# One addition in a kernel's setup: an immediate replaced by a tensor of ones

## The chip, the cores and the metric

The kernel runs on one core of one Trainium2 chip. The metric is the device time of one execution in microseconds. Timed runs of the kernel before: 690.28 us in the median of 3 runs, from 690.0 to 690.36.

## The reference, cut to what matters

A small language model tower on 64 sequences of 128 tokens, width 256: an attention layer on embedded tokens, then a gated linear recurrence, then a linear layer with the signs of a weight. The edit lies in what is computed from log_decay, the recurrence's decay.

```python
h = tok_attention(emb[x], Wq, bq, Wk, bk, Wv, bv, Wo, bo)      # 16 heads of 16
xn = layernorm(h)
Bu_proj = (xn @ B_w.T) @ C_w.T
decay = sigmoid(log_decay)                                     # (256,)
state = exclusive_scan(decay, Bu_proj)                         # over the 128 tokens
h = h + sigmoid(xn @ gate_w.T + gate_b) * state
h = h + layernorm(h) @ sign(ffn_weight).T
```

The sigmoid is computed as 1 / (1 + exp(-log_decay)), on a tile of 128 partitions x 2 columns that holds the 256 features.

## The kernel before, in words

The kernel takes the 64 sequences in 32 pairs. A software pipeline of turns runs over the pairs: turn t computes the scores and probabilities of pair t in 8 steps, while the projections of pair t+1, the context of pair t-1, the recurrence of pair t-2 and the last layer of pairs t-3 and t-4 are placed between the steps. Every engine has its own queue, written out by hand in the program's order, with semaphores between the engines; no planner changes it. Turns -2 to 5 and the last six are written out, the others are a loop.

Ahead of the turns, and inside turns -1 and 0, lies the setup. What matters here, by engine:

- **VectorE** clears small tiles (L500 to L504: powers, zero_col, eps_col and two v_wide), wraps and clips the token ids (L509 to L513) and hands them to TensorE, which turns them, and then to GpSimd (tok_ids, L515). It makes low parts of the weights wk, wq, wv (L519, L523) and centres wo. In turn -1, turn_weights follows (L539 to L557): a copy of bo_turned, the addition of one to exp(-log_decay) (L543), the reciprocal that gives decay (L545), two scans that give its powers (L549), the low part of wo (L519), a comparison of the last weight with zero (L555, with an immediate, from SBUF to SBUF) and its signs (L557). Behind it in the same queue come k_low and q_low of pair 0 (L642), gate_row (L562), state_row (L567) and the first maxima (L583).
- **GpSimd** waits for the ids, gathers embedding rows (L309), and in turns -2 and -1 clears k_stack and q_stack of one parity each (L365, L366), then copies the id columns of the next pair (L299) and gathers again.
- **ScalarE** computes exp(-log_decay) in turn_weights (L397), the high parts of weights (L382, among them woh), and k_high and q_high (L468, L480).
- **TensorE** makes the k and q features of pair 0, then in prepare (ahead of turn 0) transposes the powers (L777), waits for k_low of pair 0, and folds the centred wo into two weights: 24 matmuls, called the fold below. Then come the first scores.
- **SyncE** queues the transfers that spread k_high, k_low, q_high and q_low over k_stack and q_stack (L262, L267), each behind its part, in that order.

Of the kernel before, what the change touches and what calls it, by code (L numbers as in the profile page):

```python
# [32 lines left out]
ALU = mybir.AluOpType  # L33
# [8 lines left out]
P = 128  # L42
C = D // P
# [15 lines left out]
def build(nc, x, emb, wqT, bq, wkT, bk, wvT, bv, woT, bo, b_w, c_wT, gate_wT, gate_b, log_decay, ffn_wT, out):  # L59
    ctx = ExitStack()  # L60
    with ctx:  # L61
        def sb(name, shape, dt=fp32):
            return ctx.enter_context(nc.sbuf_tensor(name, shape, dt))
# [4 lines left out]
        def sem(name):  # L68
            return ctx.enter_context(nc.semaphore(name))
# [12 lines left out]
        e_ld, e_ld1, decay = sb("e_ld", [P, C]), sb("e_ld1", [P, C]), sb("decay", [P, C])  # L82
# [3 lines left out]
        earlier_raw, earlier = sb("earlier_raw", [P, SEQ]), sb("earlier", [P, SEQ], f32r)  # L86
        ones_col = sb("ones_col", [P, 2])
        gb_row = sb("gb_row", [P, D])
        zero_col, eps_col = sb("zero_col", [P, 1]), sb("eps_col", [P, 2])
        bv_rows, bo_row = sb("bv_rows", [P, 2, D]), sb("bo_row", [P, D])  # L90
        x_raw = sb("x_raw", [BATCH, SEQ], i32)
        x_wrap, x_sum, x_clip = (sb(n, [BATCH, SEQ]) for n in ("x_wrap", "x_sum", "x_clip"))
# [6 lines left out]
                                for n in ("xT", "ctxT", "h1T"))  # L99
# [60 lines left out]
        ids_turned, ids_ready, wstate_mm, prep_step, prep_done = (sem("ids_turned"), sem("ids_ready"), sem("wstate_mm"),  # L160
                                                      sem("prep_step"), sem("prep_done"))
# [4 lines left out]
        earlier_made, dve_gate, eps_made = sem("earlier_made"), sem("dve_gate"), sem("eps_made")  # L166
# [332 lines left out]
        def _(dve):  # L499
            nc.vector.memset(powers[:, :, 0:1], 0.5).then_inc(prep_step, 1)  # L500
            nc.vector.memset(zero_col[:], 0.0).then_inc(prep_step, 1)
            nc.vector.memset(eps_col[:], EPS).then_inc(eps_made, 1)
            for par in range(2):
                nc.vector.memset(v_wide[par][:], 0.0).then_inc(prep_step, 1)  # L504
            dve.wait_ge(prep_step, 4)
            dve.wait_ge(eps_made, 1)

            dve.wait_ge(x_loaded, 16)
            nc.vector.tensor_scalar(x_wrap[:], x_raw[:], 0.0, float(VOCAB), ALU.is_lt, ALU.mult).then_inc(ids_step, 1)  # L509
# [7 lines left out]
            def low_part(part, src, n):  # L517
                dve.wait_ge(w_high, n)
                nc.vector.tensor_tensor(part[1][:], src, part[0][:].bitcast(fp32), ALU.subtract).then_inc(w_low, 1)  # L519
# [19 lines left out]
            def turn_weights():  # L539
                dve.wait_ge(wo_flipped, 1)  # L540
                nc.vector.tensor_copy(bo_turned[:, :, 0:P], ps_t[:, D:2 * D].rearrange("p (k f) -> p k f", k=C)).then_inc(turned_copied, 1)
                dve.wait_ge(exp_ld, 1)
                nc.vector.tensor_scalar(e_ld1[:], e_ld[:], 1.0, None, ALU.add).then_inc(prep_step, 1)  # L543
                dve.wait_ge(prep_step, 5)
                nc.vector.reciprocal(decay[:], e_ld1[:]).then_inc(prep_step, 1)  # L545
                dve.wait_ge(prep_step, 6)
                for c in range(C):

                    nc.vector.tensor_tensor_scan(powers[:, c, 1:SEQ], decay[:, c:c + 1].to_broadcast([P, SEQ - 1]),  # L549
                                                 zero_col[:].to_broadcast([P, SEQ - 1]), powers[:, c, 0:1],  # L550
                                                 ALU.mult, ALU.add).then_inc(powers_made, 1)
                low_part(wo, raw[0][:], 4)
                dve.wait_ge(raw_loaded[2], 32)
                dve.wait_ge(w_low, 4)
                nc.vector.tensor_scalar(raw[0][:], raw[2][:], 0.0, None, ALU.is_lt).then_inc(prep_step, 1)  # L555
                dve.wait_ge(prep_step, 7)
                nc.vector.scalar_tensor_tensor(wf_sign[:], raw[2][:], 0.0, raw[0][:], ALU.is_gt,  # L557
                                               ALU.subtract).then_inc(prep_done, 1)
# [17 lines left out]
            def turn(t, par):  # L576
# [129 lines left out]
                if exists(t + 1):  # L706
                    if isinstance(t, int) and t == -1:
                        turn_weights()
                    split_low(k_low, g3, bk_col, k_high, act_khi, dve_klo)
# [287 lines left out]
```

## Time and profile before

| | |
|---|---|
| median of the timed runs | 690.28 us |
| profiled execution | 690.76 us |
| its span, first to last instruction | 688.7 us |
| TensorE (PE) matmul busy | 628.8 us, 91% |
| VectorE (DVE) busy | 616.4 us, 89% |
| ScalarE (ACT) busy | 592.2 us, 86% |
| GpSimd (POOL) busy | 428.4 us, 62% |
| mean granted TensorE clock | 0.988 |

The busy shares are means over the whole span. The setup lies in the first 35 us, where the shares are lower than in the steady part. Times in rows of the trace are in microseconds from the start of the span; a granted clock of 1.00 is 2.4 GHz and one of 0.50 is 1.2 GHz.

### The profile page before, as it was taken

Reading aid. Unit: us, or ns where it says so; the run is one execution under the profiler, and the core shown is the slowest. Engines: PE = TensorE matmul, PEld = TensorE weight load, DVE = VectorE, ACT = ScalarE, POOL = GpSimd, SP = SyncE. Lnnn points to the kernel's source line nnn. Section 1 sums busy time; section 2 is a strip of 40 time slices with the busy share of each in tenths; the row PEclk is TensorE's granted clock in tenths of the full one; section 3 lists DMA queues with packets and bytes.
Section 4 is the critical chain, followed back from the end, with each engine's and each line's share of the span. In section 5 each row is a group of like instructions: output and inputs, shape, how many; then the busy total and the mean of one; then the engine's idle time right before and its main releaser. Section 6 shows DMA issues by size and latency. Waiting matters only on the chain. (4 is left out here: it accounts for less than half of the span.)

```text
span 688.7 us, 21152 instructions
## 1 busy us (share of the span) xinstructions
PE 628.8 (91%) x6633; PEld 593.6 (86%) x6633; DVE 616.4 (89%) x1343; ACT 592.2 (86%) x2219; POOL 428.4 (62%) x464
## 2 busy tenths in 40 slices
PE   3678999999999999999999999999999999999772
PEld 2567989999999999999999999999999999999662
DVE  5666899999999999999999999999999999999893
ACT  3199999999999999999999999999999999999810
POOL 7401567666667676666676676666676776665595
PEclk9899999999999999999999999999999999999997
DMA  5323322233333322233443322333344322333000
GB/s 154 115 93 108 109 80 91 93 109 109 124 122 122 122 78 91 92 104 122 122 122 122 105 84 91 100 107 122 122 122 122 84 89 90 103 122 109 17 32 31
DMA packets 56162, 69.81 MB, mean 101 GB/s; under 512 B 6785, under 2 KB 41793, under 8 KB 56129
## 3 DMA queue, kind: packets, MB, share of 16 engines
q1 hardware_dynamic: 52048, 60.48, 26.8%
q0 software_dynamic: 3072, 8.39, 5.5%
q10 hardware_dynamic: 1008, 0.53, 0.3%
q8 instruction: 17, 0.28, 0.2%
q14 instruction: 17, 0.13, 0.1%
HBM read 10.65 MB, written 8.39 MB: 28 GB/s over the span
## 5 line engine op out<-in xcount | busy, mean ns | idle before, releaser
L420 ACT ACTIVATE probs<-ps_s,neg_max 128x128 f32<-128x128 f32 x1024 | 343.6, 400 | 11.4 <-DVE neg_max L583 11.4
L583 DVE TENSOR_REDUCE neg_max<-ps_s 128x4 f32<-128x512 f32 x256 | 175.6, 686 | 33.0 <-PE ps_s L750 28.9
L430 ACT COPY probsT<-ps_t 128x512 f32<-128x512 f32 x256 | 162.4, 634 | 15.9 <-PE ps_t L850 15.9
L850 PE MATMUL ps_t<-ident,probs 128*128 128x128 f32 x1024 | 156.1, 275 | 11.7 <-ACT probsT L430 10.1
L420 ACT ACTIVATION_READ_ACCUMULATOR probs<-ps_s,neg_max 128x1 f32 x640 | 157.3, 246 | 0.0
L850 PEld LDWEIGHTS ps_t<-ident,probs 128*128 128x128 f32 x1024 | 114.0, 141 | 20.5 <-issue 8.9
L750 PE MATMUL ps_s<-k_stack,q_stack 128*128 128x256 f32 x512 | 123.9, 323 | 0.0
L323 POOL TENSOR_TENSOR h<-gated,h 128x512 f32<-128x512 f32 x32 | 41.0, 1283 | 82.5 <-DVE gated L659 47.4
L360 POOL TENSOR_TENSOR mean_part<-sign_row,mean_scaled 128x512 f32<-128x512 f32 x32 | 33.3, 1041 | 93.9 <-DVE mean_scaled L736 93.8
L750 PEld LDWEIGHTS ps_s<-k_stack,q_stack 128*128 128x128 f32 x512 | 77.4, 191 | 0.1
L309 POOL DMA_INDIRECT x_emb<-in_emb,id_col x64 | 66.2, 1035 | 15.6 <-issue 14.3
L616 DVE TENSOR_REDUCE row_sum<-probs 128x4 f32<-128x512 f32 x96 | 64.7, 674 | 0.0
L750 PE MATMUL ps_c<-probsT,v_wide 128*32 128x128 f32 x2048 | 62.5, 274 | 0.0
L328 POOL TENSOR_TENSOR inv_wide<-inv_sum,ones_col 128x512 f32<-128x512 f32 x32 | 33.2, 1038 | 43.7 <-DVE inv_sum L625 28.5
L750 PEld LDWEIGHTS ps_c<-probsT,v_wide 128*32 128x32 f32 x2048 | 53.9, 110 | 4.4
L750 PE MATMUL ps_g<-woh,ctxTh 128*128 128x256 f32 x128 | 39.1, 305 | 15.3 <-DVE ctxTl L723 15.3
L598 DVE BATCH_NORM_STATS2 stats<-h 128x6 f32<-128x256 f32 x128 | 47.8, 415 | 3.4 <-POOL h L323 2.3
L315 POOL TENSOR_TENSOR rs<-ve,neg_half 128x2 f32<-128x2 f32 x64 | 46.5, 726 | 5.2 <-DVE ve L610 4.4
L750 PEld LDWEIGHTS ps_g<-woh,ctxTh 128*128 128x128 f32 x128 | 24.0, 187 | 22.8 <-DVE ctxTl L723 22.8
L356 POOL TENSOR_TENSOR state_low<-state_in,state_high 128x512 fp32r<-128x512 f32 x32 | 41.6, 1301 | 2.5
L342 POOL TENSOR_TENSOR gate_bias<-gate_bias,gb_row 128x512 f32<-128x512 f32 x32 | 41.4, 1294 | 2.5
L363 POOL TENSOR_TENSOR y_rest<-h,mean_part 128x512 f32<-128x512 f32 x32 | 41.3, 1291 | 2.5
(148 smaller groups left out, 1929.8 us busy)
## 6 DMA issues: line engine op xcount, KB each, us to landing
k_stack<-k_high SPq DMA_DIRECT2D x128, 128.0 KB, 3.5
q_stack<-q_high SPq DMA_DIRECT2D x64, 256.0 KB, 2.5
k_stack<-k_low SPq DMA_DIRECT2D x64, 128.0 KB, 3.4
q_stack<-q_low SPq DMA_DIRECT2D x32, 256.0 KB, 2.4
out<-y SPq DMA_DIRECT2D x32, 256.0 KB
x_emb<-in_emb,id_col POOLq DMA_INDIRECT x64, 3.9
raw<-in_wkT SPq DMA_DIRECT2D x1, 256.0 KB, 3.5
raw<-in_wqT SPq DMA_DIRECT2D x1, 256.0 KB, 4.2
```

The lines of the kernel that those rows point to most:

```text
L309: nc.gpsimd.indirect_dma_start(x_emb[par][b][:], None, emb, bass.IndirectOffsetOnAxis(ap=id_col[par][b][:], axis=0)).then_inc(gathered[par ...
L315: nc.gpsimd.tensor_tensor(rs[:], ve[:], neg_half[:], ALU.pow).then_inc(rs_done, 1)
L342: nc.gpsimd.tensor_tensor(gate_bias[:], gate_bias[:], gb_row[:].unsqueeze(1).to_broadcast([P, 2, D]), ALU.add).then_inc(pool_bias, 1)
L356: nc.gpsimd.tensor_tensor(state_low[:], state_in[:], state_high[:].bitcast(fp32), ALU.subtract).then_inc(state_lows, 1)
L363: nc.gpsimd.tensor_tensor(y_rest[:], h1[:], mean_part[:], ALU.subtract).then_inc(pool_rest, 1)
L420: last = nc.scalar.activation(probs[s % 2][:, j], ps_s[s % 2][:, j * SEQ:j * SEQ + SEQ], ACT.Exp, bias=neg_max[s % 2][:, j:j + 1], accum_o ...
L430: nc.scalar.copy(probsT[st][vp if st < AHEAD else 0][:], ps_t[:]).then_inc(act_pT, 1)
L583: nc.vector.tensor_reduce(neg_max[s % 2][:], ps_s[s % 2][:].rearrange("p (h k) -> p h k", h=HPS), axis=AX.X, op=ALU.max, negate=True).then ...
L598: nc.vector.bn_stats(stats[:, b], h[:, b]).then_inc(done_st, 1)
L616: nc.vector.tensor_reduce(row_sum[par][:, s // 4, s % 4 * HPS:s % 4 * HPS + HPS], probs[s % 2][:], axis=AX.X, op=ALU.add).then_inc(dve_sum, 1)
L750: return nc.tensor.matmul(dst, lhsT, rhs, start=first, stop=last)
L850: last = nc.tensor.transpose(ps_t[:, j * SEQ:j * SEQ + SEQ], probs[st % 2][:, j], ident[:])
```

## The change

A tile unit_col of 128 x 2 is added and filled with ones by a memset on VectorE, ahead of the two v_wide memsets. The wait for eps_made, behind them, is raised from 1 to 2. The addition of one at L543 is written as tensor_tensor of e_ld and unit_col instead of tensor_scalar of e_ld with the immediate 1.0. Tiles that are allocated behind unit_col may lie at other addresses.

```diff
-        zero_col, eps_col = sb("zero_col", [P, 1]), sb("eps_col", [P, 2])
+        zero_col, unit_col, eps_col = sb("zero_col", [P, 1]), sb("unit_col", [P, C]), sb("eps_col", [P, 2])
...
             nc.vector.memset(eps_col[:], EPS).then_inc(eps_made, 1)
+            nc.vector.memset(unit_col[:], 1.0).then_inc(eps_made, 1)
             for par in range(2):
                 nc.vector.memset(v_wide[par][:], 0.0).then_inc(prep_step, 1)
             dve.wait_ge(prep_step, 4)
-            dve.wait_ge(eps_made, 1)
+            dve.wait_ge(eps_made, 2)
...
                 dve.wait_ge(exp_ld, 1)
-                nc.vector.tensor_scalar(e_ld1[:], e_ld[:], 1.0, None, ALU.add).then_inc(prep_step, 1)
+                nc.vector.tensor_tensor(e_ld1[:], e_ld[:], unit_col[:], ALU.add).then_inc(prep_step, 1)
                 dve.wait_ge(prep_step, 5)
```

## Rows read from the trace of the kernel before

**Rows 1.** Stretches: PE, PEld, DVE, ACT, POOL busy (count), clock, DMA share, GB/s.

```profile
200.00:220.00 20.00, 19.48 (x210) 18.32 (x208) 18.89 (x42) 18.79 (x73) 12.90 (x14) 1.00 0.37 115
```

**Rows 2.** Order of time, VectorE's first instructions: start, duration, engine, line, operation.

```profile
0.93 0.06 DVE L502 MEMSET eps_col<- 128x2 f32 x1
...
2.32 0.96 DVE L504 MEMSET v_wide<- 128x1088 f32 x1 [0.18 <-issue]
3.32 0.22 DVE L509 TENSOR_SCALAR x_wrap<-x_raw 64x128 f32<-64x128 int32 x1
```

**Rows 3.** Order of time, the edited instruction and its followers; two ScalarE producers.

```profile
16.14 5.87 DVE L543 TENSOR_SCALAR e_ld<-e_ld 128x2 f32<-128x2 f32 x1
16.28 0.62 ACT L382 CAST woh<-raw 128x512 fp32r<-128x512 f32 x1
...
17.84 0.84 ACT L468 ACTIVATE k_high<-ps_g,bk_col 128x256 fp32r<-128x256 f32 x2 [0.94 <-PE ps_g L750]
...
22.05 0.17 DVE L545 RECIPROCAL decay<-e_ld 128x2 f32<-128x2 f32 x1
...
23.02 0.67 DVE L519 TENSOR_TENSOR wol<-raw,woh 128x512 fp32r<-128x512 f32 x1
...
23.79 0.48 DVE L555 TENSOR_SCALAR raw<-raw 128x512 f32<-128x512 f32 x1
...
24.92 0.87 DVE L642 SCALAR_TENSOR_TENSOR k_low<-ps_g,bk_col,k_high 128x256 fp32r<-128x256 f32 x2
```

**Rows 4.** Order of time, GpSimd beside the edited instruction.

```profile
16.70 3.54 POOL L365 MEMSET k_stack<- 128x4096 f32 x1
...
20.17 1.82 POOL L366 MEMSET q_stack<- 128x2048 f32 x1
...
21.92 0.31 POOL L299 COPY id_col<-tok_ids 128x1 int32<-128x1 int32 x2
```

**Rows 5.** Order of time, VectorE beside GpSimd elsewhere; last, all of L610 (min/median/max ns).

```profile
8.43 3.54 POOL L365 MEMSET k_stack<- 128x4096 f32 x1
...
10.49 0.69 DVE L519 TENSOR_TENSOR wvl<-raw,wvh 128x512 fp32r<-128x512 f32 x1 [2.87 <-ACT wvh L382]
...
90.03 1.28 POOL L323 TENSOR_TENSOR h<-gated,h 128x512 f32<-128x512 f32 x1 [9.04 <-DVE gated L659]
90.05 1.28 DVE L610 TENSOR_TENSOR ve<-mv,eps_col 128x2 f32<-128x2 f32 x1
...
382.34 1.28 POOL L323 TENSOR_TENSOR h<-gated,h 128x512 f32<-128x512 f32 x1 [2.55 <-DVE gated L659]
382.57 0.35 DVE L625 RECIPROCAL inv_sum<-row_sum 128x32 f32<-128x32 f32 x1
...
L610 DVE TENSOR_TENSOR ve<-mv,eps_col x64: 160/161/1281, 70.5 to 679.5; 128x2 f32<-128x2 f32 x64
```

**Rows 6.** Order of time, TensorE from the powers to the first scores; SyncE's last stack transfer.

```profile
23.16 0.44 PE L777 MATMUL ps_t<-ident,powers 128*128 128x128 f32 x2 [3.99 <-DVE powers L549]
...
25.94 3.75 PE L750 MATMUL ps_c<-raw,gate_in 128*128 128x256 f32 x8 [2.34 <-DVE k_low L642]
...
28.37 0.61 SPq L267 DMA_DIRECT2D q_stack<-q_low  x1
...
33.30 0.59 PE L750 MATMUL ps_s<-k_stack,q_stack 128*128 128x256 f32 x2
```

**Rows 7.** Stretches of TensorE alone: PE busy (count), granted clock, DMA share, GB/s.

```profile
19.00:23.10 4.10, 0.17 (x2) 1.00 0.42 128
...
25.94:30.90 4.96, 4.96 (x12) 0.53 0.66 226
30.90:33.30 2.40, 2.40 (x13) 1.00 0.00 0
```

**Rows 8.** Transfers into q_stack, first 60 us: issue to landing.

```profile
DMA to landing us min/median/max: 2.4/2.7/3.1
```

**Rows 9.** Waits from 12 to 40 us: total, times, longest.

```profile
ACT wgh L382 <- PE ps_g L750: 11.1, 1, 11.1
```

## The prediction

> **What bounds the kernel now.** I read the stretches of equal length first. In the middle of the run TensorE is busy 19.48 of 20 us, VectorE 18.89 and ScalarE 18.79 [rows 1]; the edited instruction isn't there. It runs once, in the setup, so the steady part doesn't change its pace and the question is by how much it starts sooner or later. For that I read the order of time of the first 35 us, engine by engine, then the waits there.
>
> In the setup one row stands out: the addition on 2 elements per partition takes 5.87 us, from 16.14 to 22.01 [rows 3], where the reciprocal of the same shape behind it takes 0.17 [rows 3] and a tensor_tensor of that shape in the loop has a median of 0.161 [rows 5]. No engine is named as what it waits for; the time is inside the instruction. Beside it GpSimd clears k_stack and q_stack of the other parity without a gap, 16.70 to 20.24 and 20.17 to 21.99 [rows 4]. The addition ends 0.02 us behind the second memset. So it is held by GpSimd's memsets, and asked before they began but did not get through.
>
> Who waits for it? VectorE's queue goes on in order: reciprocal, scans, wo's low part, comparison L555, signs L557, then k_low at 24.92 [rows 3]. TensorE's fold (the 24 matmuls of prepare) starts at 25.94 and its wait of 2.34 us is ended by k_low [rows 6]. The powers' transposes at 23.16 stand ahead of it on TensorE, also waiting for VectorE, 3.99 us [rows 6]. In turn ScalarE's wg high part waits 11.1 us for the fold [rows 9], and the first scores start as it ends, at 33.30 [rows 6]. VectorE's gate_row, state_row and first maxima come behind it by their waits in the code. So all three engines start the loop from the fold's end, and the fold hangs on the VectorE queue behind the slow addition. What moves k_low moves the whole of the rest.
>
> **The change, part by part.**
>
> The memset of unit_col (one, 2 elements): the same form as that of eps_col, 0.06 us [rows 2]. It stands ahead of the v_wide memsets, whose last ends at 3.28; x_wrap follows at 3.32 [rows 2], so nothing is idle there. Its start-to-start step among its like is 0.03. The ids, the gather and GpSimd's memsets hang on x_wrap, so all of the setup up to 21.99 may move by it: 0.03 to 0.06 us later, unless the gap ahead of the first v_wide memset hides it (then 0). I take 0.05. The second wait on eps_made costs nothing of its own: the wait for the v_wide memsets stands beside it and ends later.
>
> The addition itself: a tensor_tensor with two SBUF inputs. Was such a one ever held by a GpSimd memset? wvl<-raw,wvh, two SBUF inputs, ran at 10.49 in 0.69 us inside the k_stack memset of 8.43 to 11.97 [rows 5]; it was not held. The new instruction starts at 16.14, its price is 0.16 (median in the loop [rows 5]), end 16.30. The other bound: held until 21.99 like the old one, gain 0.
>
> The reciprocal has one SBUF input and was behind the memsets before; now it meets them. The nearest row: the reciprocal at 382.57 took 0.35, its usual time, inside the GpSimd tensor_tensor of 382.34 to 383.62 [rows 5]. So it isn't held: 0.17 as before. Bound on the other side: held until 21.99.
>
> From there the queue keeps its steps: reciprocal start to L555 start is 23.79 - 22.05 = 1.74 us [rows 3]. Reciprocal at 16.34, so wo's low part at 17.31 (woh is ready at 16.90 [rows 3]) and L555 is asked for at 16.34 + 1.74 = 18.08.
>
> L555 is a tensor_scalar on SBUF with SBUF output and an immediate, the kind of the old addition, and it now comes while the memsets run (before, it ran at 23.79, after them). I cost it as held to their end. Its 0.485 us for 512 elements against 0.67 to 0.69 for two-tensor forms of that size [rows 3, 5] says that it runs in a faster way than they do, as the kind that was held would. So L555 runs from 21.99 and ends at 22.47 in place of 24.28; L557, k_low and the fold come earlier by 23.79 - 21.99 = **1.80 us**. Bounds: if the grant comes a little before the memset's end, as the old one's 0.02 behind it suggests (0.16 of work does not fit into 0.02), 1.95; if GpSimd's id copies at 21.92 to 22.23 [rows 4] go first, 1.5. So of the 5.87 us that the stall lasts, the change takes away 5.71 and L555 gives back 3.91 (21.99 - 18.08). The other side of this: every small delay between 16.14 and 18.08 is covered by those 3.91 us.
>
> The Trainium skill (SBUF — State Buffer, "Who interferes with whom") says that copy, cast and tensor_scalar can enter the two-port modes and then block against GpSimd for the whole instruction, while a DVE instruction with two SBUF inputs contends only with a GpSimd instruction that reads SBUF. The trace agrees in both: 5.87 us beside memsets, 0.69 us inside one, and the 2-element tensor_tensor at 90.05 held 1.28 us by a GpSimd addition [rows 5]. By that rule the L555 cost above follows; by a reading without it (only the edited instruction suffers) the sum would be 5.7, the third rival below.
>
> After L555 the fold starts at 25.94 - 1.80 = 24.14. k_high is ready at 18.68 [rows 3], so nothing else is late. The stack transfers are issued in SyncE's queue behind k_low and move with it; the last, at 28.37, lands 2.4 to 3.1 later, 30.8 to 31.5, before the first scores at 33.30 [rows 6, 8]: 1.8 us of room, kept.
>
> **TensorE's clock** is the one unknown size. The fold's first 12 matmuls took 4.96 us at a granted 0.53 (1.2 GHz, the lower level), the last 12 took 2.40 at 1.00 [rows 7]; 7.36 in all. Before it TensorE had been idle from 19.17 to 23.16, worked 0.44, and idled again [rows 6, 7]. After the change the powers' transposes come right behind the q features, so one idle stretch of some 4.5 us (19.6 to 24.14) stands in place of 4.0 and 2.3. I take the clock to fall as before and to come back as long after the fold's start as before: no change. Bounds: never low, 2 x 2.40 = 4.8, a further gain of 2.56; low for the whole fold, 2 x 4.96 = 9.9, a loss of 2.56.
>
> **Sum.** -1.80 + 0.05 = -1.75 us. The profiled execution, span 688.7, took 690.76 us, and becomes 689.0. The median of the timed runs is 690.28, 0.48 lower; from it 688.5 follows.
>
> **The rivals.**
>
> 1. The clock gives more: the idle stretch is shorter in all (4.5 against 6.3 us), so TensorE doesn't fall, or comes back sooner. For: less idle time. Against: 4.0 us of idling and 0.44 of work sufficed for the fall. Gain 1.75 + 2.56 less up to 0.8, since the last stack would then land at 29.0 to 29.7 with scores wanted at 28.9: about 686.3.
>
> 2. Held all the same: the new tensor_tensor or the reciprocal waits until 21.99. For: the held row at 90.05, and no reciprocal of this kernel met a memset. Against: the rows at 10.49 and 382.57. Gain 0 to 0.15: 690.3.
>
> 3. L555 isn't held. L557 starts at 18.60, k_low at 19.21 in place of 24.92, a gain of 5.71, and as TensorE then hardly idles, up to 2.56 more for the clock: 682 to 684.6. Against: it's of the kind that was held.
>
> 4. Slower: the clock stays at its lower level through the fold and so costs 2.56 more than it did, which eats the 1.75: 691.1. It decides if the low stretch grows by more than 3.5 us, since one us of it costs half a us. For: the earlier fold might meet the clock just fallen. Against: in the trace it came back within 5 us of work, and the fold has 7.
>
> **How the numbers follow.** Chances: forecast 0.66, first rival 0.12, second 0.13, third 0.05, fourth 0.04. The forecast's own range, with the clock's return one us sooner or later (half a us each way) and the L555 bounds, is 687.7 to 689.3. The range for 8 in 10 reaches to the second rival and part of the first: 686.6 to 690.5. What a measurement can tell from no change is 0.2%, 1.38 us, so faster means under 688.9: three quarters of the forecast, and rivals one and three, 0.66. Same: the rest of it, rival two and most of four, 0.32. Slower 0.02.
>
> **What would show it.** The addition at 16.1 with about 0.16 us; the reciprocal at 16.3 with 0.17; L555 at about 18.1 lasting some 4.3 us and ending by 22.5; k_low near 23.1, the fold near 24.1, its 24 matmuls in about 7.4. An addition or reciprocal of 5.7 us shows rival two; an L555 of 0.5 us shows rival three; a granted clock of 1.00 through the fold rival one. If the fold starts 1.8 sooner but the span doesn't shrink, the claim that everything starts from the fold is wrong.

## Result: 0.4% slower, where 0.25% faster was forecast

The median of 15 runs is 692.99 us (691.53 to 694.27), that of before, measured beside them, 690.36 us (688.12 to 692.94, 15 runs). The ratio is 1.0042, with a 95% interval from 1.0028 to 1.0056. Timed again on another chip the ratio was 1.0034 (1.0018 to 1.0051). The profiled execution took 694.17 us with a span of 692.0, against 690.76 and 688.7. The measured time lies 4.5 us above the forecast and 2.5 us above its range.

Runs of either kernel fall into groups some 2 us apart, for the most part with different means of TensorE's granted clock (of the changed kernel on the second chip: six runs at 691.2 to 691.5 with a clock of 0.988 to 0.991, five at 693.6 to 694.5 with 0.982 to 0.983), so that two medians differ also by how the runs happened to fall; below, the traces carry the reasons.

**The setup after.** In order of time, the rows that answer to [rows 3] and [rows 4]:

```profile
15.92 0.15 DVE L544 TENSOR_TENSOR e_ld<-e_ld,unit_col 128x2 f32<-128x2 f32 x1
16.11 0.17 DVE L546 RECIPROCAL decay<-e_ld 128x2 f32<-128x2 f32 x1
...
17.85 4.32 DVE L556 TENSOR_SCALAR raw<-raw 128x512 f32<-128x512 f32 x1
...
22.82 0.87 DVE L643 SCALAR_TENSOR_TENSOR k_low<-ps_g,bk_col,k_high 128x256 fp32r<-128x256 f32 x2
...
20.07 1.82 POOL L366 MEMSET q_stack<- 128x2048 f32 x1
21.82 0.51 POOL L299 COPY id_col<-tok_ids 128x1 int32<-128x1 int32 x2
```

Each instruction does what was forecast: the addition takes 0.15 us, the reciprocal isn't held, the comparison is now held and takes 4.32 us. It ends at 22.17, only 0.28 us behind the second memset though its own work is 0.485 us, so it got through some 0.2 us before that memset's end (ends on GpSimd are rough in a profile). That puts k_low at 22.82, 2.10 us earlier than before, where 1.80 less 0.05 was forecast. TensorE, answering to [rows 6]:

```profile
20.04 0.38 PE L778 MATMUL ps_t<-ident,powers 128*128 128x128 f32 x2
23.83 3.75 PE L751 MATMUL ps_c<-raw,gate_in 128*128 128x256 f32 x8 [3.41 <-DVE k_low L643]
...
31.72 0.59 PE L751 MATMUL ps_s<-k_stack,q_stack 128*128 128x256 f32 x2
```

The fold starts 2.11 us earlier and takes 7.89 us for the 7.36 of [rows 7]. The first scores start at 31.72 in place of 33.30: **1.58 us gained at this point**, against 1.75 forecast. That the two agree so well is luck: the fold came 0.36 us earlier than forecast and took 0.53 us longer. By the end the kernel is 3.3 us behind. The rest is lost later, in two places.

**The clock falls once more.** Stretches of the changed kernel (PE, PEld, DVE, ACT, POOL busy, granted clock, DMA share, GB/s), then the same stretch of the kernel before:

```profile
46.00:50.00 4.00, 3.16 (x11) 2.29 (x12) 2.11 (x4) 3.60 (x18) 0.00 (x0) 0.58 0.39 145
```

```profile
46.00:50.00 4.00, 2.60 (x16) 2.00 (x16) 3.59 (x7) 3.74 (x16) 0.00 (x0) 1.00 0.66 241
```

In the stretch before it (44 to 46) TensorE was busy 0.87 of 2 us, and its waits (1.16 us ahead of 44.80, 0.65 us ahead of 46.33) were ended by ScalarE's copies of probsT. The clock then was at its lower level from 46.6 to 50.0. In the kernel before, waits of 1.21 and 0.65 us stand at the same place of the program, TensorE was busy 1.17 us from 44 to 46, and the clock stayed at 1.00. The lead over before shrinks there from 1.57 us (the row_sum of 47.9) to 0.26 us (the maximum of 51.1): 1.3 us.

**And every turn is longer.** The reciprocal of the softmax's sums (inv_sum) runs once a turn. All of it, with the first and the last start, after and before:

```profile
L626 DVE RECIPROCAL inv_sum<-row_sum x32: 340/353/356, 51.4 to 658.2; 128x32 f32<-128x32 f32 x32
```

```profile
L625 DVE RECIPROCAL inv_sum<-row_sum x32: 339/353/355, 51.7 to 654.9; 128x32 f32<-128x32 f32 x32
```

31 turns take 606.8 us for 603.2: **3.6 us lost, 0.12 us per turn**. So -1.58 + 1.3 + 3.6 = 3.3, the difference of the spans. Where in a turn? Groups of matmuls from 200 to 600 us (busy, mean ns of one), after and before:

```profile
L751 PE MATMUL ps_g<-xTl,wqh 128*128 128x256 f32 x80 | 22.6, 283 | 0.0
L751 PE MATMUL ps_g<-xTh,wkh 128*128 128x256 f32 x80 | 22.5, 282 | 0.0
L751 PE MATMUL ps_g<-wvh,xTh 128*128 128x256 f32 x84 | 23.5, 280 | 0.0
```

```profile
L750 PE MATMUL ps_g<-xTl,wqh 128*128 128x256 f32 x80 | 22.1, 276 | 0.0
L750 PE MATMUL ps_g<-xTh,wkh 128*128 128x256 f32 x81 | 22.5, 277 | 0.0
L750 PE MATMUL ps_g<-wvh,xTh 128*128 128x256 f32 x84 | 23.5, 280 | 0.0
```

The first two of each are matmuls of the k and q features, 24 per turn; the operand named first is the one that is streamed. All six of their groups grew by 4 to 7 ns; the other groups stayed within 1 or 2. Their step, the mean distance between the starts of neighbouring ones in the trace, went from 114 to 119 ns. 24 x 5.2 ns is 0.125 us per turn. Added up over the 31 turns, the steps of these matmuls grew from 82.1 to 85.7 us, and everything else that TensorE does changed by 0.1 us in all.
### The profile page after: what moved, and what is told of

Read it like the earlier page. It is cut to its first block and busy times, and to the rows that moved or that the text cites. A ratio compares the mean times of both kernels' runs of the same rounds, so it can differ in the third digit from the quotient of the medians.

```text
span 692.0 us, 21153 instructions
## 1 busy us (share of the span) xinstructions
PE 635.2 (92%) x6633; PEld 600.2 (87%) x6633; DVE 614.3 (89%) x1344; ACT 592.8 (86%) x2219; POOL 427.3 (62%) x464
## 5 line engine op out<-in xcount | busy, mean ns | idle before, releaser
L851 PEld LDWEIGHTS ps_t<-ident,probs 128*128 128x128 f32 x1024 | 115.6, 141 | 20.2 <-issue 10.8
L309 POOL DMA_INDIRECT x_emb<-in_emb,id_col x64 | 64.7, 1011 | 15.5 <-issue 14.1
```

The costliest lines, as they stand in the source:

```text
L309: nc.gpsimd.indirect_dma_start(x_emb[par][b][:], None, emb, bass.IndirectOffsetOnAxis(ap=id_col[par][b][:], axis=0)).then_inc(gathered[par ...
L851: last = nc.tensor.transpose(ps_t[:, j * SEQ:j * SEQ + SEQ], probs[st % 2][:, j], ident[:])
```

## The experiments

My theory (1): the moved tiles slow the feature matmuls. The rival: the new order of the setup shifts the engines against each other, and the steady part runs slower for it.

**unit_col last.** The changed kernel with the tile allocated behind all others:

```diff
-        zero_col, unit_col, eps_col = sb("zero_col", [P, 1]), sb("unit_col", [P, C]), sb("eps_col", [P, 2])
+        zero_col, eps_col = sb("zero_col", [P, 1]), sb("eps_col", [P, 2])
...
         y = [sb(f"y{p}", [P, 2, D]) for p in range(2)]
+        unit_col = sb("unit_col", [P, C])
```

> The changed kernel, with unit_col allocated behind all other tiles, so that every other tile lies where it lay before the change; the instructions are those of the changed kernel. Theory 1 (the new tile moves all tiles behind it by 32 bytes, and with xT 32 bytes off, the matmuls that make the k and q features run slower): the start-to-start step of those matmuls goes back from 119 to 114 ns, the drift of about 0.12 us per turn is gone, and only the setup's gain is left: a span of about 687.1 against 688.7 of before where the clock acts alike, a ratio of about 0.998. Rival (the new order of the setup shifts the engines against each other, and the steady part runs slower for it): the drift stays, span about 690.7 to 692, ratio 1.003 to 1.005.

Measured: ratio 0.9971 (0.9954 to 0.9989). The setup's rows are those of the changed kernel, and the 31 turns take 603.5 us again:

```profile
17.86 4.32 DVE L557 TENSOR_SCALAR raw<-raw 128x512 f32<-128x512 f32 x1
...
L627 DVE RECIPROCAL inv_sum<-row_sum x32: 339/354/355, 49.0 to 652.5; 128x32 f32<-128x32 f32 x32
```

The step is 114 ns. The rival falls: the same instructions in the same order have no drift.

**A tile alone.** The kernel before, `zero_col, pad_col, eps_col = ...` with an unused pad_col of [P, C] in unit_col's place:

> The kernel before with an unused tile of 128 x 2 at the place of unit_col: no instruction is changed, all tiles behind it lie 32 bytes further on. Theory 1: step of the k and q feature matmuls 119 ns, drift 0.12 us per turn, a span about 3.6 us longer than before, about 692.3 and ratio 1.005; the addition still takes 5.9 us. Rival: no drift, 688.7, ratio 1.000.

Measured: ratio 1.0053 (1.0027 to 1.0079), step 119 ns, and with no changed instruction the whole drift, 606.9 us:

```profile
L625 DVE RECIPROCAL inv_sum<-row_sum x32: 340/354/355, 52.0 to 658.9; 128x32 f32<-128x32 f32 x32
```

**Both timed on one chip,** the changed kernel and the one with unit_col last:

> The changed kernel once more, on the same chip as the next run. Its loss against before should be that of the moved tiles (3.5 us), the setup's gain in the executions in which the addition was held (1.9 us in about a third of them), and the clock: a median 2 to 3.5 us above before. If the loss were in the new instruction, the next run would show it too.

> The changed kernel with unit_col last, on the same chip as the run before: a median 3.5 to 5 us below it, and 0 to 2 us below before. If only the clock's distribution had made its first result good, it would be within 1 us of after.

Measured: 691.53 (691.15 to 694.48) and 689.43 (687.32 to 690.76) beside 690.06 of before; ratios 1.0034 (1.0018 to 1.0051) and 0.9988 (0.9972 to 1.0003). The medians differ by 2.1 us, less than the 3.5 to 5 expected: six of 11 runs of the first lie within 0.4 us of its fastest, five of 12 of the second within 0.8 us. The fastest ones differ by 3.8 us, and the traces by the drift: 607.0 against 603.2 us for 31 turns. The two timings of the instruction change by itself gave 0.3% and 0.1%, the second not clear of nothing.

**Which place matters?** Five layouts, one execution of each (ten of the first):

```diff
+        zero_col, unit_col, pad_col, eps_col = ...        # changed kernel, 64 bytes
+        xT = ...; pad_col = sb("pad_col", [P, C]); ctxT, h1T = ...   # before, pad behind xT
+        pad_col = sb("pad_col", [P, C]); raw = ...        # before, pad ahead of all weights
+        xT = ...; decay = sb("decay", [P, C]); ctxT, h1T = ...       # before, decay moved behind xT
+        zero_col, pad_col, eps_col = ..., sb("pad_col", [P, 32]), ...   # before, 128 bytes
```

> The changed kernel with one more unused tile of 128 x 2 behind unit_col: the later tiles lie 64 bytes further on than before the change, not 32. Theory 1a (what counts is where a tile lies modulo 64 bytes): step 114 ns, as the run with unit_col last, ratio about 0.998. Theory 1b (any move away from the old places costs): step 119 ns, ratio about 1.004.

> The kernel before with an unused tile of 128 x 2 behind the two xT tiles: xT stays at its place, ctxT, h1T and all that follows lie 32 bytes further on. If the place of xT itself, the moving operand of the k and q feature matmuls, sets their step, it stays at 114 ns and nothing drifts (less than 0.02 us per turn). If one of the tiles behind it does (the tiles that the other engines write at that time), the step is 119 ns and a turn 0.12 us longer.

> The kernel before with an unused tile of 128 x 2 ahead of the raw tiles: all weights and xT move by 32 bytes together, and their distance is as before. If the distance of the two operands counts, the step of the k and q feature matmuls is 114 ns as before. If the place of each by itself counts (xT then lies where it lay in the changed kernel), it is 119 ns, a turn 0.12 us longer.

> The kernel before with the tile decay allocated behind xT instead of ahead of powers: xT and the tiles between lie 32 bytes lower, weights and all tiles behind xT stay. If the distance between xT and its neighbours on either side sets the step of the k and q feature matmuls, it leaves 114 ns for 117 to 120, with a drift of 0.07 to 0.15 us per turn. If only moves to higher addresses or only the tiles behind xT do it, the step stays at 114.

> The kernel before with an unused tile of 128 bytes at the place of unit_col: all tiles behind it lie 128 bytes further on, after 32 and 64 were tried. If a longer period than 64 bytes exists and is 128, the step is back at 114 ns; if the slow step comes with any such move, it is 119 to 120 ns and the drift 0.12 to 0.14 us per turn.

Measured (step of the feature matmuls; last minus first start of the inv_sum reciprocal):

```
                              step ns      31 turns us
before, three traces          114          603.2, 603.5  (662.5 on the last chip)
unit_col, 32 bytes            119          606.8, 607.0  (664.5)
pad alone, 32 bytes           119          606.9
unit_col and pad, 64 bytes    119 to 120   607.5
pad behind xT                 k 115, q 117 604.9
pad ahead of the weights      114 to 115   603.6
xT 32 bytes lower             118 to 119   (664.0)
pad of 128 bytes              118          (663.1)
```

The kernel moved by 64 bytes had a ratio of 1.0046 (1.0028 to 1.0063). The numbers in brackets come from another chip, on which every kernel took some 750 us, as TensorE idled for its own issue within the 32-column matmuls; there they compare only with each other. Three drifts on it are smaller than expected: 2.0 us for the changed kernel where 3.7 was, 1.4 with xT lower (at least 2.2 expected) and 0.6 with the pad of 128 bytes (at least 3.7). The idling takes up part of the slow step: it was 31.7 us in all in the kernel before and 30.2 in the changed one. With the pad of 128 bytes the matmuls that stream a weight had shorter steps (115 to 117 ns), which gave back 0.8 us in 31 turns.

Theory 1a (the place modulo 64 bytes) fell: 64 and 128 bytes are slow too. What stays fast is the old distance between weights and xT: when all moved together, nothing changed; when xT alone with small tiles came 32 bytes lower, the step was slow. But a pad behind xT, which leaves both operands in place, also cost 4 ns on the q features, which neither outcome of its expectation had. So the distance of the two operands goes with most of the slow step of these 24 matmuls, not with all of it, and each layout was traced once or twice. It is no rule for the others: those that stream a weight kept their 116 to 118 ns when their distance changed by the same 32 bytes, and most took 119 to 120 with 64 bytes and 115 to 117 with 128.

**The matmuls by themselves.** A program of these 24 matmuls only, the weights and the streamed tile as far apart as in the kernel, the streamed operand at 0, 32, 64 and 128 bytes in turn, the other engines first idle, then busy:

> Not the kernel's computation: only the 24 matmuls of a turn's k and q features, over and over, on tiles of 0.5 that lie to each other as the weights and xT do (distance 42,688 bytes), with the moving operand 0, 32, 64 and 128 bytes further on in turn; first with the other engines idle, then with ScalarE copying, VectorE reducing and GpSimd multiplying. It leaves out all the rest and writes one block of zeros. If the distance of the two operands alone sets the step, the first part shows 114 ns at 0 and about 119 to 120 at 32 and 64. If the slow step comes from the other engines' reads and writes, all four offsets show about 109 ns (as the transposes in the kernel do) in the first part and differ in the second. If only the whole kernel's layout makes it, neither part shows a difference.

Measured, steps in ns for 0, 32, 64, 128 bytes: 113.3, 118.1, 119.7, 118.0 in the first round with the others idle, 117.6, 118.3, 119.7, 118.0 in every later round, idle or busy alike, at a granted clock of 1.00. The first moved operand comes at 17.99 (a row "x2" holds two neighbours; three matmuls take 0.34 us before it and 0.36 behind it):

```profile
17.31 0.39 PE L135 MATMUL ps_g<-xt,wqh 128*128 128x256 f32 x2
17.54 0.28 PE L135 MATMUL ps_g<-xt,wql 128*128 128x256 f32 x1
17.65 0.39 PE L135 MATMUL ps_g<-xt,wqh 128*128 128x256 f32 x2
...
18.34 0.40 PE L135 MATMUL ps_g<-xt,wkh 128*128 128x256 f32 x2
18.58 0.28 PE L135 MATMUL ps_g<-xt,wkl 128*128 128x256 f32 x1
18.70 0.40 PE L135 MATMUL ps_g<-xt,wkh 128*128 128x256 f32 x2
```

Neither "about 109 at all offsets" nor "no difference" came. The slow step comes with all other engines idle, and they add nothing to it when they work. What I did not expect: offset 0 is fast only until a moved operand has been streamed, and takes 117.6 afterwards in an unbroken run of matmuls. The fast step ends with the first moved matmuls, but this is seen once; in the later rounds the four offsets differ by some 2 ns. So this program shows the slow step without the rest of the kernel, and not that the distance alone decides. In the kernel before, the features come behind transposes and scores in every turn, and are back at 113.4 ns from the third of a group of 12 on. What keeps the step slow in one and not in the other, and why a pad behind xT costs something, was not tested.

**Which tensor_scalar is held?** The kernel before again, twice, and the changed kernel again:

> The kernel before, unchanged, for a second trace: which part of its time depends on when TensorE's clock falls and comes back. Expected: VectorE's setup rows as in the first trace (the addition about 5.9 us, k_low near 24.9), no drift between the two traces over the steady turns, and a span that differs from 688.7 by up to 2.6 us with the stretches at a granted clock of 0.50 in the first 60 us and by nothing else.

> The kernel before, a third trace. Two traces of it differ in which tensor_scalar GpSimd holds: the addition (5.87 us, issued 0.38 us after the start of the second gather) or, where VectorE came earlier (issued 0.16 us before it), the comparison (4.73 us). Expected: one of the two, never both; k_low at 24.9 if the addition is held and near 23.0 if not.

> The changed kernel, a second trace: the addition at 0.15 us and the comparison held to GpSimd's end again, k_low near 22.8, the drift over the steady turns 0.12 us per turn as in the first trace; the second fall of the clock near 46.6 may be absent, and the span is then shorter by 1.3.

The first of these expectations failed in the row on which my forecast rests, and so the clock is not all that differs between two traces of one kernel. The second trace of before:

```profile
15.69 0.16 DVE L543 TENSOR_SCALAR e_ld<-e_ld 128x2 f32<-128x2 f32 x1
...
17.63 4.73 DVE L555 TENSOR_SCALAR raw<-raw 128x512 f32<-128x512 f32 x1
...
23.00 0.87 DVE L642 SCALAR_TENSOR_TENSOR k_low<-ps_g,bk_col,k_high 128x256 fp32r<-128x256 f32 x2
...
15.85 0.95 POOL L309 DMA_INDIRECT x_emb<-in_emb,id_col  x1 [0.31 <-issue]
16.79 3.54 POOL L365 MEMSET k_stack<- 128x4096 f32 x1
```

**Here the old addition is not held at all**: it takes 0.16 us, the comparison is held instead, and k_low starts at 23.00, like the changed kernel's 22.82. In the third trace it is the same (addition 0.16, k_low 22.95). Over all eight traces of kernels with the old addition it was held in two. In these it was issued 0.38 us after the start of GpSimd's second gather of turn -1; in the six others 0.19 us after it or earlier. In the held ones the first memset began only 0.56 us later, so something shut it out before any memset ran. GpSimd was in the gather then; by these times the gather shuts a tensor_scalar out from some point between 0.19 and 0.38 us after its start on, and the memsets follow without a gap. (The changed kernel's reciprocal, issued 0.44 us after that start, was not held, nor was its tensor_tensor at 0.25.) The closest comparison is in the last run below, where the addition as tensor_tensor was issued at the same 0.38 us as in the two held cases, and ran:

```profile
15.74 0.95 POOL L311 DMA_INDIRECT x_emb<-in_emb,id_col  x1 [0.30 <-issue]
...
16.12 0.15 DVE L551 TENSOR_TENSOR e_ld<-e_ld,unit_col 128x2 f32<-128x2 f32 x1
```

A few tenths of a us of the setup's timing decide. The changed kernel's second trace was as expected in the setup (0.15, 4.32, k_low 22.69) but had the second fall of the clock as well; its drift was 2.0 us in 31 turns (664.5 against 662.5), half of what was expected, on the slow chip.

**The comparison as tensor_tensor,** which answers what L555 gives back:

```diff
-                nc.vector.tensor_scalar(raw[0][:], raw[2][:], 0.0, None, ALU.is_lt).then_inc(prep_step, 1)
+                nc.vector.tensor_tensor(raw[0][:], raw[2][:], zero_col[:].unsqueeze(1).to_broadcast([P, C, D]), ALU.is_lt).then_inc(prep_step, 1)
```

> The changed kernel with unit_col last, and the comparison of the last weight with zero (L556 of the changed kernel) written as tensor_tensor against a broadcast column of zeros. If that comparison is what gives back 3.9 of the 5.7 us that the addition no longer loses, it takes 0.69 us instead of 4.32, k_low comes at about 19.2 instead of 22.8, and the fold about 3.6 us earlier; span about 683 to 684 where the clock acts alike. If k_low or the fold is bound by something else just behind, less than half of this is gained.

```profile
17.76 0.69 DVE L557 TENSOR_TENSOR raw<-raw,zero_col 128x512 f32<-128x512 f32 x1
...
20.11 1.97 PE L752 MATMUL ps_c<-raw,gate_in 128*128 128x256 f32 x8
...
24.43 0.65 SPq L268 DMA_DIRECT2D q_stack<-q_low  x1
29.36 0.79 PE L752 MATMUL ps_s<-k_stack,q_stack 128*128 128x256 f32 x2 [3.84 <-DMA q_stack<-q_low]
```

Measured: ratio 0.9942 (0.9916 to 0.9968), span 685.5. The comparison and k_low (19.09) came as forecast, the fold started at 20.11, the clock did not fall before its end, and it took 5.1 us. But TensorE then waited 3.84 us for the last stack transfer. Of 3.7 us that the fold is earlier than in the run with unit_col last (23.84), and some 1.7 that it is shorter, the first scores keep 1.2 (29.36 for 30.59), and the span of 685.5 misses the 683 to 684 expected. From 28.8 to 32.2, behind most of this wait, the granted clock was 0.50. The next bound is the row of nine stack transfers: the last is issued at 24.43 and lands 4.9 us later.

**The first q_high transfers on ScalarE's queue:** `act.dma_start(q_stack[0][row:P:4]..., q_high...)` for rows 0 and 2 behind q_high in turn -1, and left out of SyncE's list there.

> The kernel with unit_col last and the comparison as tensor_tensor, and with the two first transfers of q_high into q_stack issued by ScalarE's queue instead of SyncE's. In the run without this the fold ended near 25.2 and TensorE then waited 3.84 us for the last stack transfer, issued at 24.43. If SyncE's issuing in order is what binds there, that last issue comes about 1.3 us earlier and the first scores 1.3 to 3 us earlier than 29.36, the span 1 to 2.5 us shorter than 685.5 where the clock acts alike. If the transfers' own time binds (they share the queues), the scores stay near 29.

```profile
23.90 0.61 SPq L269 DMA_DIRECT2D q_stack<-q_low  x1
...
28.03 0.51 PE L758 MATMUL ps_s<-k_stack,q_stack 128*128 128x256 f32 x2 [2.21 <-DMA q_stack<-q_low]
```

Measured: ratio 0.9945 (0.9925 to 0.9965), span 682.5, 3 us below the run before, the scores 1.33 us earlier. The last issue moved by 0.5 us only, where 1.3 was expected if SyncE's order alone bound, and it landed after 4.1 us instead of 4.9; so the transfers' own time binds too. Another 1.3 us of the 3 come until the first inv_sum (45.51 for 48.15): the clock did not fall in this trace. The ratios of the two, from different chips, can't be told apart; both beat the kernel before and the changed one.

## Why the prediction was wrong, by its own steps

1. **"The steady part doesn't change its pace": wrong, and this is the loss.** The step took the edit for one instruction and put the new tile's effect on the layout at nothing without a reason, though the tile lies in the middle of it. Its place costs 24 x 5.2 ns in each turn, 3.6 us in 31 of them, shown by the tile alone (slow without the edit) and by the edit without the move (fast). By what mechanism the place does it stays open. No rival held it; the fourth, the only one on the slow side, was the clock.
2. **"The addition takes 5.87 us": true of two executions in eight.** The mechanism (a tensor_scalar held by GpSimd, a tensor_tensor not, the comparison held in its place) was right, with 3.8 us given back for 3.91 and k_low 2.1 us earlier for 1.75. One detail was not: the addition was shut out before GpSimd's memsets began, beside the gather. But the second and third traces of before have k_low at 23.0 already. With the held execution in two of eight traces, a gain of 1.9 to 2.1 us is perhaps 0.5 us in the mean (an estimate from two in eight), and the kernel with unit_col last gained 0.3% and 0.1% in its two timings.
3. **The fold at its old 7.36 us: 7.89.** Within the stated bounds of 4.8 and 9.9. The second trace of before had it at 6.6 and the first with unit_col last at 6.8, with less of it at the lower clock.
4. **Everything starts from the fold: right up to 47 us,** where the lead of 1.57 us was whole. Then came a second fall of the clock, 1.3 us, in turn 0. It is in three traces of the changed kernel and of four others (once with unit_col last), and in none of the three of before. Whether the edit makes it likelier isn't shown.
5. The memset: x_wrap at 3.35 for 3.32, 0.03 us, at the lower end. The wait costs nothing.
6. Rivals one to three were wrong as put: the clock was at 0.50 in the fold, neither the addition nor the reciprocal was held, and the comparison was. But rival two's outcome, no gain, is what k_low shows in the other two traces of before. Rival four had the direction, slower, but by a clock that stays low through the fold; it was low for 5.7 of the 7.89 us and cost 0.53, not 2.56.

## What to carry to other kernels

Put a new tile, however small, at the end of the layout, or compare the edit with a kernel that has the tile and not the edit: here 8 bytes per partition cost more than the edit could give. A stall of one instruction in one profile is a sample, not a price: where it depends on which of two engines comes first by tenths of a us, take several traces before counting it. And where a stall is held by another engine's work, look for the next instruction of the same kind behind it; it inherits the stall.

## What the runs showed of the hardware that was not expected

- Where the tiles lie in SBUF changes the step of a matmul at a granted clock of 1.00: the k and q features, 256 columns each, took 114 ns at the kernel's own layout and 118 to 120 with the streamed operand 32, 64 or 128 bytes further from the weights. The slow step came with all other engines idle too. It was 114 again when weights and streamed operand moved together.
- In an unbroken run of these matmuls the slow step persisted: the same layout took 113.3 ns ahead of the moved operands and 117.6 after them.
- The kernel's other matmuls of 256 columns, which stream a weight, took 116 to 118 ns before and after the change, mostly 119 to 120 with the tiles 64 bytes further on, and 115 to 117 with 128.
- A tensor_scalar of 2 elements per partition took 5.87 us in both cases in which it was issued 0.38 us after the start of a GpSimd indirect DMA with memsets behind it, and 0.16 us in the six in which it was issued up to 0.19 us after that start. A tensor_tensor of the same shape, issued at 0.38 us, took 0.15.
- One chip took 745 to 749 us for kernels that take 686 to 692 us elsewhere; TensorE stood idle 34 us in all ahead of its 32-column matmuls there, 31.7 of them for its own issue.
